# Head-by-head DRAM layout of the key and query parts, and 16-row loads of their high parts, in three attention stages

## What is computed

```python
v = (value @ Wv.T + bv).reshape(n, -1, H, D)
k = (key @ Wk.T + bk).reshape(n, -1, H, D)
q = (query @ Wq.T + bq).reshape(n, -1, H, D)
qk = jnp.einsum('nqhd,nkhd->nhqk', q, k)          # a0: masked; a3: a mask is added
attn = jax.nn.softmax(qk * scale, axis=3)
out = jnp.einsum('nhqk,nkhd->nqhd', attn, v).reshape(n, q_len, H * D)
x = x + out @ Wo.T + bo
```

## Time and profile before

| | before |
|---|---|
| median of 3 runs | 4700.8 us |
| the profiled execution | 4706.5 us |
| its span, first to last instruction | 4704.8 us |
| TensorE busy | 3914.7 us (83%) |
| VectorE busy | 3099.6 us (66%) |
| ScalarE busy | 2060.3 us (44%) |
| GpSimd busy | 796.3 us (17%) |
| granted TensorE clock, mean | 0.896 of full speed |
| stage a0: first block, second block | 10 to 175 us, 175 to 828 us |
| stage a2: first block, second block | 2925 to 3080 us, 3080 to 3525 us |
| stage a3: first block, second block | 3831 to 3987 us, 3987 to 4433 us |

### The profile page before, as it was taken

One profiled execution on the slowest core, in us unless ns is written; L12 is line 12 of the kernel. 1 busy time (PEld: TensorE's weight loads), 2 busy tenths in 40 slices (PEclk: granted clock), 3 DMA queues, 4 the chain that ended last, 5 costly groups with the idle time before them and its releaser, 6 DMA issues. The chain is left out here.

```text
span 4704.8 us, 82799 instructions
## 1 busy us (share of the span) xinstructions
PE 3914.7 (83%) x30525; PEld 2826.9 (60%) x30525; DVE 3099.6 (66%) x7110; ACT 2060.3 (44%) x3636; POOL 796.3 (17%) x510
## 2 busy tenths in 40 slices
PE   6599999699367999785499996669988974999899
PEld 5244444588365777674388885535555663455577
DVE  7466664546656666545466664668867884988687
ACT  2155555134113333342154443247776851677511
POOL 4333330501341000000023323210000021000000
PEclk8699999599668999897599998869998997899999
DMA  6333331201320000010244545412210024121100
GB/s 205 102 98 101 101 96 41 88 21 44 106 77 32 18 18 18 28 43 31 72 126 123 130 125 144 166 60 66 67 37 14 1 71 148 55 66 65 34 19 19
DMA packets 202874, 337.94 MB, mean 72 GB/s; under 512 B 26036, under 2 KB 119781, under 8 KB 202566
## 3 DMA queue, kind: packets, MB, share of 16 engines
q1 hardware_dynamic: 186680, 306.61, 20.4%
q0 software_dynamic: 15888, 27.23, 2.8%
HBM read 242.42 MB, written 107.01 MB: 74 GB/s over the span
## 5 line engine op out<-in xcount | busy, mean ns | idle before, releaser
L1904 ACT ACTIVATE a_pT<-a_psS 128x512 f32<-128x512 f32 x1536 | 835.9, 598 | 405.0 <-PE a_psS L1790 399.6
L1976 DVE TENSOR_REDUCE a_mx<-a_psA 128x1 f32<-128x512 f32 x1024 | 656.6, 685 | 88.1 <-PE a_psA L1768 87.8
L1768 PE MATMUL a_psA<-a_ks,a_qs 48*128 48x512 f32 (+1 forms) x1536 | 404.4, 522 | 160.9 <-PEq L46 59.0
L1805 PE MATMUL a_psZ<-a_pT,a_V 128*17 128x128 f32 x12288 | 488.4, 278 | 0.0
L1972 DVE CUSTOM_DVE_ANT_0 a_scored<-a_psA,a_hide_q 128x512 bf16<-128x512 f32 x512 | 332.6, 688 | 193.4 <-PE a_psA L1768 192.3
L1805 PEld LDWEIGHTS a_psZ<-a_pT,a_V 128*17 128x17 f32 x12288 | 272.6, 97 | 270.8 <-issue 161.7
L1768 PEld LDWEIGHTS a_psA<-a_ks,a_qs 48*128 48x128 f32 (+1 forms) x1536 | 151.2, 192 | 408.7 <-issue 176.0
L1790 PE MATMUL a_psS<-a_qs,a_ks 50*128 50x512 f32 (+1 forms) x1536 | 319.1, 409 | 3.2 <-ACT a_pT L1904 0.8
L3244 DVE SCALAR_TENSOR_TENSOR ex_h<-ex_psU,ex_ub,ex_sg 128x512 f32<-128x512 f32 x129 | 96.9, 751 | 188.6 <-PE ex_psU L159 181.6
L1988 POOL TENSOR_TENSOR X<-X,a_osb 128x512 f32<-128x512 f32 x48 | 61.2, 1280 | 941.1 <-ACT a_osb L1891 923.1
L3190 ACT CAST ex_w_h<-X 128x1024 fp32r<-128x1024 f32 x102 | 106.1, 1041 | 149.3 <-DMA X<-in_L_ffn_gw 145.3
(11 more groups left out here) (606 smaller groups left out, 10257.4 us busy)
## 6 DMA issues: line engine op xcount, KB each, us to landing
a_k_parts<-a_p_kp SPq DMA_DIRECT2D x96, 256.0 KB
a_q_parts<-a_p_qp SPq DMA_DIRECT2D x96, 256.0 KB
a_qs<-a_q_parts SPq DMA_DIRECT2D x192, 128.0 KB
a_ks<-a_k_parts SPq DMA_DIRECT2D x192, 128.0 KB
X<-in_L_ffn_gw SPq DMA_DIRECT2D x36, 512.0 KB, 4.5
X<-in_L_ffn_up_w SPq DMA_DIRECT2D x36, 512.0 KB, 3.3
X<-in_L_ffn_down_w SPq DMA_DIRECT2D x36, 512.0 KB, 3.8
top_rows<-blank_rows SPq DMA_DIRECT2D x32, 514.0 KB, 11.3
```

Source lines behind the costliest of these rows:

```text
L1768: nc.tensor.matmul(psA[:, unit(a, par) % 3], qs[r, g % ring, p % 2, q * P:(q + 1) * P], ks[r, g % ring, p % 2], start=True, stop=True).the ...
L1805: last = nc.tensor.matmul(psZ[q * VP:q * VP + VW, g % 2, j * P:(j + 1) * P], V[:, b, kt, g % NG * GH + j, :], pT[:, p % 2, par, kt, q * P: ...
L1904: nc.scalar.activation(pT[:, p % 2, par, kt, :], psS[:, unit(t, par) % 3], ACT.Exp).then_inc(exp_done, 1)
L1976: nc.vector.tensor_reduce(mx[:, p // 2 % 2, par, p % 2, q:q + 1], psA[:, unit(a, par) % 3], AX_X, ALU.max).then_inc(a_used, 1)
```

## The change

The two DRAM tensors are laid out as [part, batch, head, d, token]. A store's 128 rows are then one contiguous run of DRAM, and its DRAM pattern goes over 128 rows of 2 KB where it went over 8 heads of 16 rows. In `load_group` every third of a stack gets a DMA of its own with 16 rows of two heads (16 x 2 x 2 KB, 64 KB); the doubled high part comes as two such DMAs in place of one broadcast of 128 KB. A group has 12 such loads where it had 8 (in a3 two more for the mask, as before), with the same bytes.

```diff
-                            heads = dram[n, :, m * P // DH:(m + 1) * P // DH].rearrange("d h t -> h d t")
+                            heads = dram[n, m * P // DH:(m + 1) * P // DH].rearrange("h d t -> (h d) t")
                             sp.dma_start(heads, parts[:, n, m].bitcast(F32)).then_inc(stored, 16)
...
-    LOADS = 2 * (4 + (added is not None))
+    LOADS = 2 * (6 + (added is not None))
...
-        q_dram = nc.dram_tensor(nm + "q_parts", [2, B, DH, H, S], F32).ap()
-        k_dram = nc.dram_tensor(nm + "k_parts", [2, B, DH, H, S], F32).ap()
+        q_dram = nc.dram_tensor(nm + "q_parts", [2, B, H, DH, S], F32).ap()
+        k_dram = nc.dram_tensor(nm + "k_parts", [2, B, H, DH, S], F32).ap()
...
-                    return dram[part:part + 1, b, :, first:first + 2].rearrange("r d h t -> r d (h t)")
-
-                for stack, start, src in ((qs, 0, heads(q_dram, 0).to_broadcast([2, DH, 2 * S])), (qs, 2 * DH, heads(q_dram, 1)),
-                                          (ks, 0, heads(k_dram, 1)), (ks, DH, heads(k_dram, 0).to_broadcast([2, DH, 2 * S]))):
-                    rows = slice(64 * par + start, 64 * par + start + src.shape[0] * DH)
-                    sp.dma_start(stack[rows, slot].bitcast(F32).rearrange("p j t -> p (j t)"), src).then_inc(group_loaded[slot], 16)
+                    return dram[part, b, first:first + 2].rearrange("h d t -> d h t")
+
+                for stack, third, src in ((qs, 0, heads(q_dram, 0)), (qs, 1, heads(q_dram, 0)), (qs, 2, heads(q_dram, 1)),
+                                          (ks, 0, heads(k_dram, 1)), (ks, 1, heads(k_dram, 0)), (ks, 2, heads(k_dram, 0))):
+                    rows = slice(64 * par + third * DH, 64 * par + (third + 1) * DH)
+                    sp.dma_start(stack[rows, slot].bitcast(F32), src).then_inc(group_loaded[slot], 16)
```

## The result

The changed kernel takes 4569.5 us (median of 4 runs, 4566.8 to 4573.8) against 4702.5 us for the kernel before beside it (4 runs): ratio 0.9713, interval 0.9692 to 0.9733. The forecast was 4571 us. Five more runs gave 4572.5 us and 0.9707 (0.969 to 0.9724).

What follows compares the result with a forecast made beforehand. Two DMA engines shared by broadcasts and stores were taken as the bound. Gains of 41.6 (a2), 41 (a3), 34 (a0) and 13 (second blocks) sum to 129.6 us, giving 4571 us against 4700.8; range 4540 to 4620 us.

Steps and rivals of the forecast that it cites:

- two engines carry both kinds: First block, late batch: broadcasts (10.1 us) and stores (10.6 us) add up to 20.7 us on two shared DMA engines.
- the first blocks: From the first key low part to the second block: gains of 41.6 us in a2, 41 in a3, 34 in a0.
- Stores on 16 engines: A batch's 2.1 MB of stores take 5.3 or 6.8 us in place of 10.6; issuing eight takes 4.8 us.
- Twelve loads: A group's 16-row loads cost 6.6 us on all engines, at 0.55 us each; issue 5.8 to 7.4 us.
- rival of the narrow door: 16-row loads hold engines up and stores queue behind them: late batch 15.1 us, 4600 us in all; chance 0.09.
- Late rounds: a2's first block, two rounds to 3032.15: 35.7 us becomes 25, at 12.5 us each; gains 10.7.
- Early rounds: a2's first block, four rounds to 2996.42: 50.7 us becomes 44.8, at 11.2 us each; gains 5.9.
- The block's end: a2's first block, from 3032.15 to the second block at 3080.32: 48.2 us becomes 23; gains 25.
- a0: Its first block of 140.8 us, with GpSimd waiting for mask loads behind stores, gains 34 us.
- Its four steps: a0's first block, to 72.45, the first mask, the second mask, the second block: gains 3.7, 7.8, 9.5 and 13 us.
- The second blocks: TensorE's waits for loaded stacks go: gains 7 us in a0 and 6 in a3, 13 together; none in a2.
- Everything else: The rest of the span outside the first and second blocks: forecast gain 0.

Runs made afterwards that it cites:

- Each half alone: Two kernels with half the change against the kernel before: only the stores on 16 engines, 4626.1 us (0.9821); only the loads on 16 engines, 4661.3 us (0.9907).

## Why the prediction was right, and where its terms were off

*The mechanism: two engines carry both kinds.* Shown. Each half alone left the other's signature (late rounds of 15 to 16 us with two engines at the end on the broadcasts; a share of 0.51 under the stores of outermost size 8), and a second buffer that took away 106 of 152 us of ScalarE's waits gave 6 us.

*How close the number came.* 4571 against 4569.5 us is partly luck. By the spans the gain was 136.5 us where the terms gave 129.6; by the medians it was 133.0, and the forecast started from the median of three runs, 1.7 us lower than that of the four beside the changed kernel. Of the terms, the first blocks were each 2 to 4 us short.

*Stores on 16 engines.* 404 GB/s with the loads beside them, the faster of the two bounds that I had taken (twice 198, 5.3 us a batch). Eight stores were set at 4.8 us of issue; the cheapest store took 0.32 us and the median of the key stores 0.44, but the eight of the late batch shown above took 5.3, so the term was about right there.

*Twelve loads.* This is the term of the late batch that was mis-sized: 6.6 us of transfer in a sum of 13.6. By themselves they take 5.6 us, and those are issue, not transfer: 64 KB per 0.465 us at a share of 0.48. Stores, loads and context of a batch together are 3.4 MB, 8.4 us at 404 GB/s (an estimate), less than VectorE's round. The 0.55 us that I had read off a 16-row load came from a window of 0.6 us in which broadcasts shared the engines. The rival of the narrow door rested on the same row; it wanted 15.1 us for a late batch, and in a2 and a3 none took over 11. The issue was read wrongly too: I had put 0.44 against 0.58 us down to 16 and 32 pieces per load. The new loads have 32 pieces of 2 KB and took 0.42 us (median), as the 16 pieces of 4 KB did in the old layout. The Trainium skill's section on the DMA port swizzle (SBUF — State Buffer) gives 104 GB/s for 16 neighbouring partitions, measured with 1 MiB. Here the six thirds of a half cover 48 rows between them and moved 138 GB/s while SP's issue set the pace, so no run here shows such a limit.

*Late rounds.* 12.5 us each forecast, 10.9 measured: 3.2 us more gain in a2 than my 10.7. The round equals that of the early batches, which have no loads, and VectorE is idle for only 0.4 us in the one from 2950.26, so it is VectorE's. SP's 11.3 us for a whole late batch stand right beside it, and 24 loads pushed the round over it.

*Early rounds.* 5.9 us forecast, 4.8 measured. The first one after the block's start is 12.7 us in place of my 11.2. It was 12.7 before as well, and is so in a2 and a3 of every kernel here, so it was never a wait for stores; what sets it is open.

*The block's end.* 23 us forecast; 23.05 in a2 and 23.6 in a3.

*a0.* 34 forecast, 37.6 measured. Its four steps became 32.9, 12.2, 29.9 and 28.1 us where 34.5, 12.5, 29.3 and 30.6 stood. The masks' path, two of the four steps, was still late after the change: moving them took another 14 us.

*The second blocks.* The sum was right (13 forecast, 12.2 measured), and its parts look wrong: a0 7.6 for 7, but a2 4.1 where I had 0, and a3 0.5 where I had 6, though TensorE's waits for stacks went in a3 as forecast. The difference lies in TensorE's granted clock at the start of the block. The first 60 us of the second block of a3 in the changed kernel, of a3 in its second profiled execution, of a2 in the changed kernel, and of a2 and a3 before:

```profile
3854.00:3914.00 60.00, 43.85 (x316) 19.73 (x316) 46.84 (x78) 20.55 (x39) 18.47 (x8) 0.55 0.15 42
```

```profile
3865.40:3925.40 60.00, 43.86 (x399) 20.63 (x400) 52.05 (x86) 24.95 (x49) 18.37 (x8) 0.66 0.18 48
```

```profile
2995.00:3055.00 60.00, 43.94 (x388) 20.45 (x392) 51.38 (x85) 24.32 (x47) 18.37 (x8) 0.65 0.15 45
```

```profile
3080.30:3140.30 60.00, 44.12 (x307) 19.90 (x311) 46.30 (x77) 19.93 (x38) 18.39 (x8) 0.54 0.13 40
...
3987.00:4047.00 60.00, 43.88 (x400) 20.72 (x400) 52.23 (x86) 25.12 (x49) 18.33 (x8) 0.67 0.14 45
```

TensorE is busy for the same 44 us in all five, but does 307 to 316 matmuls in the slower kind and 388 to 400 in the other. Both kinds occur with both kernels, so it isn't the change: a2 went from the slower kind to the faster, and a3 the other way. Like is to be set beside like. Among the second blocks of the faster kind, a2 took 437.0 us with broadcasts (the kernel with two buffers) and 435 to 440 with twelve loads in five traces; a3 took 438.8 to 446.6 with broadcasts in three traces and 435.6 to 440.4 with twelve loads in five, 5 us less on average. That fits the forecast's 0 and 6 as well as a spread of 4 us can, so the 4.1 and the 0.5 are chance around them.

*Everything else* came to -1.7 us, where I had put nothing.

## What to carry to other kernels

Count the DMA engines that each transfer uses (share and GB/s of a short window in which it is alone) before believing that the DMA side is half idle: a mean share of 0.49 hid two engines that were full. Then add up the time of all kinds on the engines they share; removing the wait by another buffer gave 6 of 4707 us while that sum stood. Splitting a narrow transfer into wide ones costs issues on the queue, and the price of that is decided where the queue is next needed in time: here 6.9 us of issue in a group of 12.5 cost nothing that shows, and 13.3 us made the kernel 108 us slower, some 75 of them in the second blocks.

## What the runs showed of the hardware that I had not expected

- After the meeting at the end of the first block, in which TensorE stands idle (12.7 us in a2 of the changed kernel), it starts the second one at 1.2 GHz (granted clock 0.5). In otherwise equal work the mean over the block's first 60 us is either 0.54 to 0.57 or 0.65 to 0.69 in the 22 second blocks of a2 and a3 of the 11 traces. The two kinds part at the rise to 2.4 GHz: from 36 to 48 us after the start the granted clock is 0.50 in a2 before and 0.83 in a3 before, with TensorE busy for 12.0 and 11.9 of these 12 us. By the maxima of the fourth group the slower kind is 5 to 6 us behind (59.6 and 58.9 us against 53.5 and 53.6). Two executions of one and the same kernel differed by 2.4 to 5.9 us in a second block that fell into different kinds. What decides the kind is open.
- The issue of a DMA of the same bytes depends on its pattern. A store of 256 KB takes 0.57 us at the least with outermost size 8, contiguous runs or not, and from 0.32 us with 128 rows. A load of 64 KB in 32 pieces of 2 KB takes 0.42 us (median) with outermost size 16, and at least 0.58 us as a broadcast with outermost size 2. The store row of the changed kernel, to set beside the earlier trace rows, and the row of the broadcasts of the kernel with only the stores on 16 engines:

```profile
L1400 SPq DMA_DIRECT2D a_k_parts<-a_p_kp x96: 319/444/1544, 35.6 to 3846.7; - x96
L1597 SPq DMA_DIRECT2D a_qs<-a_q_parts x384: 580/600/1111, 82.4 to 4286.8; - x192
```
